# Between the stages of a six-stage kernel: one meeting of the engines in place of two, semaphores cleared beside the next stage, no drain of GpSimd's queue

## What is computed

```python
def _forward(v, q, adj, ...):                       # stages 1 and 2
    self_feat = concat([v, q_exp]) @ W_self.T + b_self
    output = self_feat
    for d in range(2):
        A = adj_f if d == 0 else swapaxes(adj_f, 1, 2)
        output = output + _gat_attention(self_feat, A.sum(-1), A @ w_bias + b_bias, ...)   # 16 heads, 20 columns
    return v + relu(output)
...
mod = silu(c) @ W_mod + b_mod                       # stage 1
x = x + g_msa * _attention(_modulate(_layernorm(x), sh_msa, sc_msa), W_qkv, W_out, b_out)  # stages 3, 4 and 5
x = x + g_mlp * _ff(_modulate(_layernorm(x), sh_mlp, sc_mlp), W1, b1, W2, b2)              # stage 6
```

## Time and profile before

| | us |
|---|---|
| median of 3 runs | 3224.87 (3224.06 to 3225.6) |
| the profiled execution, its own time | 3222.87 |
| its span, first to last instruction | 3221.1 |
| PE busy in it | 3076.9 |
| POOL busy in it | 845.7 |

### The profile page before, as it was taken

How to read it: one execution, slowest core, us unless ns; L and a number is a source line. 1 busy time by engine, 2 the same in 40 slices (tenths; PEclk the granted TensorE clock), 3 DMA queues, 4 the chain that set the end, 5 groups by cost and what they waited for, 6 DMA issues and landing times. The chain is left out here.

```text
span 3221.1 us, 62151 instructions
## 1 busy us (share of the span) xinstructions
PE 3076.9 (96%) x24696; PEld 2440.8 (76%) x24696; DVE 1850.5 (57%) x2743; ACT 1341.9 (42%) x2786; POOL 845.7 (26%) x571
## 2 busy tenths in 40 slices
PE   8969998999999799999999999999896999999999
PEld 5968887888888577777777777777685888888887
DVE  4357785212211388888888888888564334333432
ACT  2145653222222277777777777777002111111111
POOL 1011112100000143444444344436454111111110
PEclk9989998999999899999999999999997999999999
DMA  4554222333332333233333333332563001010100
GB/s 140 178 183 145 96 70 97 107 106 104 104 114 102 105 110 96 80 94 92 94 80 93 92 94 81 92 97 70 215 241 111 1 27 33 26 33 26 33 14 14
DMA packets 196342, 297.28 MB, mean 92 GB/s; under 512 B 27889, under 2 KB 105713, under 8 KB 194055
## 3 DMA queue, kind: packets, MB, share of 16 engines
q1 hardware_dynamic: 182528, 276.54, 27.6%
q0 software_dynamic: 4288, 14.68, 1.3%
q10 hardware_dynamic: 9296, 2.77, 0.4%
HBM read 190.44 MB, written 103.49 MB: 91 GB/s over the span
## 5 line engine op out<-in xcount | busy, mean ns | idle before, releaser
L1338 DVE TENSOR_REDUCE b_nm<-b_ps 128x1 f32<-128x1024 f32 x512 | 601.6, 1216 | 16.3 <-PE b_ps L1279 3.2
L1245 ACT ACTIVATE b_p<-b_ps,b_nm 128x1024 f32<-128x1024 f32 x512 | 565.0, 1113 | 40.8 <-DVE b_nm L1338 40.8
L1308 PE MATMUL b_po<-b_pt,b_v 128*64 128x256 f32 x4096 | 498.3, 385 | 0.8 <-DVE b_pt L1358 0.8
L1250 ACT ACTIVATE b_pt<-b_tp_act 128x512 f32<-128x512 f32 x512 | 308.6, 603 | 305.1 <-PE b_tp_dve L1291 305.1
L1358 DVE COPY b_pt<-b_tp_dve 128x512 f32<-128x512 f32 x512 | 351.2, 686 | 117.3 <-PE b_tp_dve L1291 117.2
L1291 PEld LDWEIGHTS b_tp_act<-ident,b_p 64*128 64x128 f32 x4096 | 312.2, 138 | 128.8 <-issue 100.6
L1308 PEld LDWEIGHTS b_po<-b_pt,b_v 128*64 128x64 f32 x4096 | 271.9, 136 | 128.6 <-ACT b_pt L1250 0.9
L1291 PE MATMUL b_tp_act<-ident,b_p 64*128 64x64 f32 x4096 | 347.8, 225 | 2.4 <-issue 2.4
L1291 PE MATMUL b_tp_dve<-ident,b_p 64*128 64x64 f32 x4096 | 347.7, 225 | 0.0
L1700 ACT ACTIVATE d_ge<-d_pf,d_b 128x512 f32<-128x512 f32 x128 | 88.2, 689 | 596.6 <-PE d_pf L1722 596.6
L1291 PEld LDWEIGHTS b_tp_dve<-ident,b_p 64*128 64x128 f32 x4096 | 311.8, 138 | 2.4
(11 more groups left out here) (253 smaller groups left out, 5666.8 us busy)
## 6 DMA issues: line engine op xcount, KB each, us to landing
b_raw_q<-q_t SPq DMA_DIRECT2D x128, 256.0 KB, 4.3
q_t<-p_qk SPq DMA_DIRECT2D x64, 256.0 KB, 2.0
k_t<-p_qk SPq DMA_DIRECT2D x64, 256.0 KB, 2.0
v_n<-p_vs SPq DMA_DIRECT2D x32, 512.0 KB, 3.2
b_raw_k<-k_t SPq DMA_DIRECT2D x128, 128.0 KB, 4.2
b_v<-v_n SPq DMA_DIRECT2D x32, 512.0 KB, 3.9
b_rb<-inv SPq DMA_DIRECT2D x64, 256.0 KB, 3.8
o_t<-b_ot SPq DMA_DIRECT2D x32, 512.0 KB, 2.6
```

What stands on the lines that cost most here:

```text
L1245: act.activation(pr[k % 4][:], ps[k % 2][:], ACT.Exp, bias=nm[:, k % 4:k % 4 + 1], accum_out=rs[:, n:n + 1]).then_inc(exp_done, 1)
L1250: act.activation(dst, src, ACT.Copy).then_inc(t_out[0], 1)
L1308: mm = pe.matmul(po[rows, (blk % 2) * 2 * P:(blk % 2 + 1) * 2 * P], vt[u][:, kc, rows], pt[blk % 2][h][:, kc, :], start=(kc == 0), stop=(k ...
L1338: dve.tensor_reduce(nm[:, k % 4:k % 4 + 1], ps[k % 2][:], axis=AX.X, op=ALU.max, negate=True).then_inc(max_done, 1)
```

## The change

In all six stages the second meeting goes, and the clears are written as range clears alone, without a drain ahead of each. Semaphores are released uncleared, so the next stage gets other numbers, and GpSimd clears the old ones after the one meeting, on its own, while the other engines enter the next stage. The two `w_mod_in` semaphores of the first stage are cleared one by one. Each block is opened with `no_gpsimd_drain=True`, so that GpSimd comes to the meeting without a drain. In the graph stage SyncE issues the stores of `y`, that of tile k - 4 ahead of the load of `x` for tile k, and waits for them at the end.

```diff
-def sems(ctx, nc, prefix, names, first=False):
+def sems(ctx, nc, prefix, names):
     handles = [nc.alloc_semaphore(prefix + "_" + n) for n in names.split()]
 
     def clear():
-        nc.clear_and_free_semaphores(handles)
-        if first:
-            nc.all_engine_barrier()
+        numbers = sorted(h.num for h in handles)
+        for low in [n for n in numbers if n - 1 not in numbers]:
+            high = low
+            while high in numbers:
+                high += 1
+            nc.gpsimd.sem_clear(range(low, high))
+        for h in handles:
+            nc.release_semaphore(h)
...
-        w_mod_in = sems(ctx, nc, "tables", "w_mod_in0 w_mod_in1")
-        block = ctx.enter_context(nc.Block())
+        w_mod_in = [nc.alloc_semaphore("tables_w_mod_in%d" % i) for i in range(2)]
+        for h in w_mod_in:
+            ctx.callback(nc.gpsimd.sem_clear, h)
+        block = ctx.enter_context(nc.Block(no_gpsimd_drain=True))
...
+            def store(k):
+                sp.wait_ge(y_done, k + 1)
+                sp.dma_start(y[k * P:(k + 1) * P, :], yo[k % 2][:]).then_inc(y_out[k % 2], 16)
+
             def turn(i):
                 for j in range(TT):
                     k = i * TT + j
+                    if k >= 4:
+                        store(k - 4)
                     sp.wait_ge(x_free, k + 1)
...
             for i in range(B * BT // TT):
                 turn(i)
+            for k in range(B * BT - 4, B * BT):
+                store(k)
+            for n in range(2):
+                sp.wait_ge(y_out[n], 16 * B * BT // 2)
...
                 pool.sem_inc(x_free, 1)
-                pool.dma_start(y[k * P:(k + 1) * P, :], yo[k % 2][:]).then_inc(y_out[k % 2], 16)
...
-            for n in range(2):
-                pool.wait_ge(y_out[n], 16 * B * BT // 2)
```

More of the change, by code:

```diff
@@ L126, in graph_tables @@
             ctx, nc, "tables", "x_in ws_in ct_in w_in s_in pool_done dve_step xt_done xt_copied sf_done sf_copied kh_done kb_written "
[L127 removed]
+            "g_done g_rounded q_done gp_done gh_rounded gl_done cg_done cg_written pn_done pn_copied out_done")
         (id_ready, b_mod_in, silu_done, mod_done, mod_t_done, gates_done, gates_copied) = sems(
@@ L441, in graph_attention @@
             ctx, nc, "graph", "st_in ws_done zeros_set dve_step rs_done xt_done xh_copied xl_done o_done a_done adj_used lg_done sub_done "
-            "exp_done p_done wt_done wt_copied pv_done relu_done y_done x_free w_in", first=True)
+            "exp_done p_done wt_done wt_copied pv_done relu_done y_done x_free w_in")
         x_in = sems(ctx, nc, "graph", " ".join("x_in%d" % i for i in range(4)))
@@ L858, in projections @@
             ctx, nc, "proj", "w_split ln_step half_set var_ready rstd_ready z_done t_done xm_done rounded x_split mb_done "
-            "m_done qk_done v_done w_rounded qk_free v_free", first=True)
+            "m_done qk_done v_done w_rounded qk_free v_free")
         w_in, ones_set = sems(ctx, nc, "proj", "w_in ones_set")
@@ L1107, in attention @@
             ctx, nc, "attn", "q_in ones_set raw_used rounded qk_ready s_done max_done exp_done inv_done inv_turned inv_stored rb_in "
-            "t_done av_done o_out o_scaled o_stored o_free first_split ri_clear", first=True)
+            "t_done av_done o_out o_scaled o_stored o_free first_split ri_clear")
         t_out = sems(ctx, nc, "attn", "t_out0 t_out1")
@@ L1408, in output_projection @@
         (rounded, o_split, m_done, gated_done, bias_done, y_bias, y_done) = sems(
-            ctx, nc, "outproj", "rounded o_split m_done gated_done bias_done y_bias y_done", first=True)
+            ctx, nc, "outproj", "rounded o_split m_done gated_done bias_done y_bias y_done")
         w1_in, = sems(ctx, nc, "outproj", "w1_in")
@@ L1569, in mlp @@
             "t_done xm_done rounded x_split f1_done gelu_done g_rounded g_split f2_done o_done gated_done "
-            "bias_done y_bias y_done", first=True)
+            "bias_done y_bias y_done")
         w2_in = sems(ctx, nc, "mlp", " ".join("w2_in%d" % i for i in range(NP2)))
```

## The result

The changed kernel takes 3215.73 us, median of 10 runs (3214.51 to 3218.62). The kernel before takes 3225.23 in the same comparison (10 runs, 3223.91 to 3226.93). The ratio is 0.9972, with a 95% interval of 0.9962 to 0.9981: faster by 0.28%, 9.5 us. The prediction was 3215.2.

A forecast was written before the change was run, and what follows sets the result against it. Inside stages TensorE bounds the kernel (96% busy); only standstill at the six stage ends can go. Terms 6.2 - 0.15 + 2.9 + 0.7 = 9.7 us saved take the median 3224.87 to 3215.2, range 3211.5 to 3220.0.

The forecast's parts named there:

- the tables' border: From tables to graph stage: 0.9 us saved, taken between POOL's constants 0.7 us earlier and ACT's table loads 1.3 us earlier.
- Second meetings, 6.2: Five borders between stages: dropping the second meeting saves 5.3 us at four and 0.9 at the graph stage's start.
- End of the graph stage, 2.9: Behind the last addition: POOL's 2.66 us drain goes, and SP's last store lands 0.3 us faster than POOL's.
- the projections' 1.7: Border from graph stage to projections: the second meeting's share there, 1.7 us of the 6.2.
- The meeting's new form, -0.15: Drain and arrival become two instructions, costing 0.03 us at each of five borders.
- End of the program, 0.7: Behind the last release: ten clears, 0.8 us, replace seven drain-and-clear pairs and the second meeting, saving 0.7 us.
- that rival: Clears may wait like a drain, 0.18 us each: graph border gives 0.3 less, the end 0.7 less, 3216.2; within main case.
- Stores on SP's queue, 0: Graph stage: SP's 32 added stores cost nothing, as the loads delayed 0.4 us are used over a tile (11.6 us) later.
- the rival of SP's queue: Graph stage: late stores of y stop ACT and PE, up to 3255 us; chance of any slower result 0.04.
- Borders give little: Second meetings may hide code fetch, so five borders give nothing, 3221.3, or half, 3218.3; together 0.19.
- The clock at the projections: A shorter PE pause at the projections' start leaves the clock at 2.4 GHz, 2.6 us more won, 3212.6; chance 0.09.
- the clock's slow stretch: At five borders PE's half-clock time may begin at another point: about 1 us in the main case's range.

The follow-up runs named there:

- e7: The changed kernel with one more semaphore-only meeting of the five engines behind GpSimd's clears in each of the six stages; 3218.88 us, ratio 0.9979.
- e2: The kernel before with only the no_gpsimd_drain=True option added in all six stages; 3223.16 us, ratio 0.9993 (interval includes 1).
- e3: The kernel before with only the stores of y moved to SP's queue, both meetings and GpSimd's drain kept; 3221.93 us, ratio 0.9992 (interval includes 1).
- e4: The changed kernel with GpSimd's drain put back in all six stages; 3221.45 us, ratio 0.9989.
- e11: The changed kernel with SP's store of tile k-4 issued behind the loads of x and adj of tile k; 3215.59 us, ratio 0.9971.
- e6: The changed kernel with its 4 MB load of w_qk_raw cut into four loads of 1 MB, one every fourth tile; 3210.45 us, ratio 0.9956.
- e12: The changed kernel with w_qk_raw in four loads and SP's stores behind the loads of x and adj; 3209.53 us, ratio 0.9952.
- e8: The changed kernel with GpSimd's drain back in every stage and ten already satisfied waits added on PE at program start; 3212.43 us, ratio 0.9962.
- e1: The changed kernel with GpSimd's drain and its stores of y put back; 3222.31 us, ratio 0.9996 (interval includes 1).

## Why the prediction was right, step by step

The time came within 0.5 us of the forecast, and the mechanism was the forecast one: the gain lies at the borders. That the number is so close is in part luck. The sum was 9.7, and the six borders gave 10.9 in the profiled pair, because two terms were too small (the tables' border and the program's end) and one was missing (GpSimd's step to its own issue). Against it stands time inside the stages that the sum put at nothing.

- *Second meetings, 6.2.* The border behind the tables is 1.3 us shorter, the others but the graph stage's 1.1, 1.2 and 1.1; expected 0.9, 1.2, 1.2 and 1.2. The first was mis-sized: between POOL's 0.7 and the table loads' 1.3 the loads won (`a_x_copy` and PE's first matmul 1.4 us earlier). e7 shows what such a meeting costs without drains, 4.3 us in all.
- *End of the graph stage, 2.9, with the projections' 1.7.* 4.6 expected, 5.15 measured (7.73 to 2.58). The 0.59 us between POOL's last addition and its own DMA issue was missed: a row of before that I had not brought into the sum. That the drain's 2.66 us stand on the path was right (e2). What the prediction did not see is that they are there only with POOL's own stores ahead, so that one of the two edits would have been enough (e3, e4).
- *The meeting's new form, -0.15.* e4, with one semaphore instruction less at each meeting, has 0.4 us less over six borders; mis-sized by little, if it is that instruction.
- *End of the program, 0.7.* 1.0 measured. Ten clears take 0.8 us, as worked out; the clears do not wait as a pair does, so that rival falls.
- *Stores on SP's queue, 0.* ScalarE never waits for `y`, so the rival of SP's queue falls. But "what waits behind them is used more than a tile later" failed at tile 7: there `x` is waited for in both kernels, 2.1 and 3.2 us. The prediction had named a wait of ACT for `x` as a sign that it is wrong, and this step of it is. Of the 2.3 us that the stage is ahead by then, 1.1 is given back there in the profiled pair, and more to the clock that is at half behind the pause, though e2 shows that such a wait differs by as much from profile to profile. The step took the cover, the time in which a late load costs nothing, from the mean tile period, 11.6 us, and not from the row of the tile behind the 4 MB. The store itself was not the cause (e11). With the load cut up the loss is gone (e6, e12).
- *Borders give little.* Falls: 0.1 us from release to first DMA at every border.
- *The clock at the projections.* Falls: half clock for 5.0 us behind a pause of 5.2, as for 5.3 behind one of 10.4.

The profiled pair differs by 7.8 us and not 10.9, because the stages between their borders took 3.1 us more: 0.7 the graph stage, 0.6 each the attention and the output projection, and 1.7 the mlp, less 0.4 in the projections. The mlp's 1.7 can be read. PE's clock rises some 30 us into that stage in both kernels, and in the changed one it falls once more, from about 2482 to 2485 us, behind a pause of 2.8 us (2.0 in before). The windows of the changed kernel, and of before at about the same distance from the stage's start:

```profile
2480.00:2486.00 6.00, 4.22 (x12) 0.72 0.01 3
```

```profile
2488.00:2494.00 6.00, 4.01 (x18) 1.00 0.00 1
```

A mean of 0.72 over 6 us is 3.4 us at half clock, and so 1.7 us lost. The change is not what brings it: the changed kernel's repeat and e2, which has before's mlp, have the second fall too (0.73, and 0.79 over 8 us), and e8, whose borders are the changed kernel's but for the drain, has none. It is the term "the clock's slow stretch", which the prediction had at about 1 in its range. The graph stage's part is less than what the same code varies by (363.4 in before, 365.9 in e2). The attention's and the output projection's are inside the spread of all the profiles here (1170 to 1171.5 and 181.9 to 183.4 us), and no run settles them.

## What to carry to other kernels

Ask of a drain what its engine has issued ahead of it: GpSimd's cost 2.67 us here behind its own stores and 0.04 without them. Two edits that remove the same wait are worth it only once. A border between stages can be read to 0.1 us in a profile, so price its edits there, and if the median says something else, look in the stages that the edit did not touch: the code queue's packet count, PE waits that end on "issue", and the granted clock. A large load in one piece can make the small loads behind it late: here four loads of 1 MB in place of one of 4 MB shortened the stage by 3.3 us, or by 4.9 against the repeat. And before a microsecond inside a stage is put down to an edit, look at how much that stage differs between two profiles of the same code.

## What was not expected of the hardware

Ten satisfied waits on PE at the start of the program changed the time of a loop 2.4 ms later: 190 code packets or 172, pauses of 2.0 and 2.4 us or none, medians 3.4 us under before against 11.6, and 2.5 against 6.8. And a drain of GpSimd took 2.67 us with its own last store just landed (e1), 0.04 us in the same stage without stores of its own (e4).
